# Column scores of a pooled attention on Trainium2: eight one-row transposes of a copied row in place of eight products, and new orders on four engines

## What is computed

```python
x = x + L0(x)   # zX*laplace_x + zY*laplace_y + zR*x*(1-x), per-batch scalars, reflected borders
x = x + L1(x)   # pooled attention, below
x = x + L2(x)   # x @ W[subject].T + b[subject], W one of eight 512x512
x = x + L3(x)   # adapter: z = relu(x@Wd + bd); y = x + z@Wu + bu; layer norm * g + b

def L1(hidden):
    attn_in = tanh(einsum('bsd,da->bsa', hidden, W1) + b1)     # a = 128
    scores = einsum('bsa,a->bs', attn_in, v)                   # one score per row of x
    mask = l <= j, l >= j or l != j, by the batch's token      # 1024 x 1024
    p = softmax(where(mask, scores[:, None, :], -1e30), axis=-1)
    return einsum('bjl,bld->bjd', p, hidden) / count(mask)
```

## Time and profile before

| | us |
|---|---|
| median of 3 runs | 558.15 |
| lowest, highest run | 556.75, 558.15 |
| the profiled execution, whole | 555.42 |
| its span in the trace | 553.6 |
| TensorE busy | 530.6 (96%) |
| VectorE busy | 467.9 (85%) |
| ScalarE, GpSimd busy | 312.3, 311.0 (56% each) |
| mean share of full TensorE clock granted | 0.992 |

### The profile page before, as it was taken

One profiled execution on the slowest core, in us unless ns is written; L12 is line 12 of the kernel. 1 busy time (PEld: TensorE's weight loads), 2 busy tenths in 40 slices (PEclk: granted clock), 3 DMA queues, 4 the chain that ended last, 5 costly groups with the idle time before them and its releaser, 6 DMA issues.

```text
span 553.6 us, 8994 instructions
## 1 busy us (share of the span) xinstructions
PE 530.6 (96%) x2838; PEld 417.1 (75%) x2838; DVE 467.9 (85%) x1164; ACT 312.3 (56%) x545; POOL 311.0 (56%) x283
## 2 busy tenths in 40 slices
PE   8996789999999999999999999999999999999995
PEld 3565576988688876888778885888778886888783
DVE  6548795999799997999889996999979998787677
ACT  5644663477635774576654775367655676335520
POOL 5156713597266944598275962589355872246241
PEclk9997999999999999999999999999999999999999
DMA  7974665585997579973898659965998847422563
GB/s 249 312 191 76 180 219 171 109 175 103 282 308 163 114 190 318 261 140 102 260 317 189 143 142 313 269 141 106 236 331 194 171 98 212 58 58 57 115 90 120
DMA packets 63942, 100.83 MB, mean 182 GB/s; under 512 B 10894, under 2 KB 16526, under 8 KB 63895
## 3 DMA queue, kind: packets, MB, share of 16 engines
q0 software_dynamic: 16544, 29.90, 33.0%
q1 hardware_dynamic: 38096, 53.54, 30.2%
q10 hardware_dynamic: 9254, 16.81, 8.0%
HBM read 67.43 MB, written 31.98 MB: 180 GB/s over the span
## 4 chain that ended last, share of the span: by engine, by line
PE 84%; DVE 7%; ACT 4%; issue 3%; POOL 1%; DMA 1%; ACTq 0%; DVEq 0%
PE y L697 37%; PE front_ps L755 10%; PE front_ps L836 8%; PE front_ps L697 6%; PE front_ps L778 5%; PE front_ps L711 4%; PE front_ps L763 3%; PE front_ps L769 2%; PE front_ps L800 2%; DVE x2f L1555 2%; ACT zh L1140 2%; DVE pn L1509 1%; PE front_ps L810 1%; PE front_ps L782 1%; PE y L737 1%
## 5 line engine op out<-in xcount | busy, mean ns | idle before, releaser
L583 POOL TENSOR_TENSOR norm<-norm 128x1 f32<-128x1 f32 x64 | 51.3, 801 | 150.5 <-DVE norm L1582 149.7
L697 PE MATMUL y<-wth,x2h 128*128 128x512 f32 x256 | 104.0, 406 | 0.0
L697 PE MATMUL y<-wth,x2l 128*128 128x512 f32 x256 | 100.2, 392 | 0.0
L697 PE MATMUL y<-wtl,x2h 128*128 128x512 f32 x256 | 100.0, 391 | 0.0
L601 POOL TENSOR_TENSOR x2l<-x2f,x2h 128x1024 fp32r<-128x1024 f32 x32 | 76.8, 2400 | 14.6 <-ACT x2h L1017 14.4
L564 POOL TENSOR_TENSOR xd<-xn 128x1024 f32<-128x1024 f32 x28 | 54.7, 1954 | 44.2 <-DVE x L1428 22.7
L1555 DVE SCALAR_TENSOR_TENSOR x2f<-alb,small,front_ps 128x128 f32<-128x128 f32 x256 | 70.7, 344 | 1.7 <-POOL x2l L601 0.4
L836 PEld LDWEIGHTS front_ps<-th_pt,x 128*128 128x128 f32 x512 | 62.0, 190 | 6.9 <-DVE x2f L1555 4.1
L836 PE MATMUL front_ps<-th_pt,x 128*128 128x129 f32 x512 | 64.7, 278 | 2.5 <-DVE x2f L1555 1.0
L590 POOL DMA_DIRECT2D out<-o_sb x58 | 57.1, 1056 | 8.1 <-ACT o_sb L1157 7.1
L1017 ACT ACTIVATE x2h<-x2f 128x1024 fp32r<-128x1024 f32 x32 | 34.0, 1062 | 46.6 <-DVE x2f L1555 46.6
(11 more groups left out here) (138 smaller groups left out, 1092.3 us busy)
## 6 DMA issues: line engine op xcount, KB each, us to landing
xn<-in_x SPq DMA_DIRECT2D x32, 512.0 KB, 7.7
out<-x ACTq DMA_DIRECT2D x58, 256.0 KB, 4.0
out<-o_sb POOLq DMA_DIRECT2D x58, 256.0 KB, 6.4
xu<-in_x SPq DMA_DIRECT2D x21, 512.0 KB, 7.8
xu<-in_x POOLq DMA_DIRECT2D x21, 512.0 KB, 7.6
wn_wd<-in_L_cond_weight SPq DMA_DIRECT2D x8, 1024.0 KB, 6.6
wn_wd<-in_L_cond_down_w SPq DMA_DIRECT2D x8, 256.0 KB, 6.6
up_row<-in_L_cond_up_b SPq DMA_DIRECT2D x8, 256.0 KB, 4.3
```

The lines of the kernel that those rows point to most:

```text
L583: pool.tensor_tensor(rstd[:, r:r + 1], ve[:, r:r + 1], minus_half[:, :], ALU.pow).then_inc(rstd_ready, 1)
L697: ins = mm(dst, lhs, rhs, start=first and q == 0, stop=last and q == len(parts) - 1, skip_group_check=True)
```

## The change

`scores_by_row` no longer multiplies. ScalarE copies the first partition of the spread scores, 1 by 512 for each half, from PSUM into the first partition of `th`, once VectorE has read that half (`sb_read`), so `th` is no longer needed there; TensorE turns the row into eight columns, with a 1x1 identity, once both halves are copied (`score_kept`). In `steady` it comes one `linear` later than before. All four compute engines' lists are written in a new order, in `opening`, `first`, `steady` and `last`; no other step changes what it does, and SyncE's list stays in its order (a helper only takes the test for the last batch).

```diff
+        score_kept = sem("score_kept")
...
             def scores_by_row(n):
-                pe.wait_ge(th_ready, 2 * n + 2)
+
+                pe.wait_ge(score_kept, 2 * n + 2)
                 for j in range(NJ):
-                    ins = mm(SN[:, j:j + 1], th[:, blk(j)], v_col[:, :], start=True, stop=True)
+                    ins = pe.transpose(SN[:, j:j + 1], th[0:1, blk(j)], ident[0:1, 0:1])
                 ins.then_inc(sn_ps, 1)
...
+            def keep_scores(n, h):
+
+                act.wait_ge(sb_read, 2 * n + h + 1)
+                copy(th[0:1, half(h)], pair_b[0:1, half(h)]).then_inc(score_kept, 1)
```

TensorE, the lists of `opening`, `steady` and `last`:

```diff
                 spread_scores(0, 0)
                 spread_scores(0, 1)
                 scores_by_row(0)
+                block_sums(0)
                 down_through_w(0)
-                block_sums(0)
                 transpose_p(0, 0)
...
                 linear(b, 1 - q, 7)
+                adapter_up(b, 1 - q, 6)
                 transpose_w(n, 0)
-                adapter_up(b, 1 - q, 6)
                 adapter_down(n, q)
                 adapter_up(b, 1 - q, 7)
+                if m is not None:
+                    transpose_x1(m, 1 - q, 0)
                 transpose_w(n, 1)
-                if m is not None:
-                    transpose_x1(m, 1 - q, 0)
                 transpose_w(n, 2)
...
                     spread_scores(m, 0)
                     spread_scores(m, 1)
+                linear(n, q, 2)
+                if m is not None:
                     scores_by_row(m)
-                linear(n, q, 2)
+                linear(n, q, 3)
                 if m is not None:
                     block_sums(m)
                     down_through_w(m)
-                linear(n, q, 3)
+                adapter_up(n, q, 2)
                 if m is not None:
                     transpose_p(m, 0)
-                adapter_up(n, q, 2)
...
                 adapter_up(LAST, 1, 5)
+                linear(LAST, 1, 7)
                 adapter_up(LAST, 1, 6)
-                linear(LAST, 1, 7)
                 adapter_up(LAST, 1, 7)
```

ScalarE, the start and the middle of `steady`, and its end:

```diff
+                small_exps(n)
                 if m is not None:
                     reflect(m, 0)
-                small_exps(n)
+                row_exps(n)
+                store_base(b, 2)
+                round_v(n)
+                seed(b, 4)
+                keep_p(n, 0)
+                keep_p(n, 1)
...
                 adapter_relu(n, 1)
+                store_base(b, 7)
                 round_w(n, 1)
                 round_w(n, 2)
...
-                store_base(b, 6)
-                store_base(b, 7)
...
                     hidden(m, 1)
+                    keep_scores(m, 0)
                 scale(n, 0)
                 if m is not None:
+                    keep_scores(m, 1)
```

More of the change, by code:

```diff
@@ L609, in first @@
             def first():
-                rest_difference(0)
+                start_sum(0)
                 add_below(1, 0)
+                rest_up(0, 0)
                 add_below(1, 1)
@@ L616, in first @@
                 add_below(1, 2)
-                add_below(1, 3)
                 left_and_right(1, 2)
-                start_sum(0)
-                rest_up(0, 0)
+                rest_difference(0)
                 rest_x2(0, 0, 0)
@@ L624, in first @@
                 rest_x2(0, 0, 3)
+                add_below(1, 3)
                 left_and_right(1, 3)
@@ L628, in steady @@
             def steady(b, n, m, q):
+                start_sum(n)
+                rest_up(n, q)
                 if m is not None:
                     left_and_right(m, 0)
+                rest_difference(n)
+                if m is not None:
                     add_below(m, 0)
                     add_below(m, 1)
+                finish(b, 0)
                 root(b, 1)
-                finish(b, 0)
+                if m is not None:
+                    add_below(m, 2)
+                root(b, 2)
                 if m is not None:
                     left_and_right(m, 1)
-                rest_up(n, q)
-                root(b, 2)
-                rest_difference(n)
-                if m is not None:
-                    add_below(m, 2)
-                start_sum(n)
+                    add_below(m, 3)
+                rest_x2(n, q, 0)
                 root(b, 3)
                 finish(b, 1)
-                rest_x2(n, q, 0)
-                if m is not None:
-                    add_below(m, 3)
+                rest_x2(n, q, 1)
                 finish(b, 2)
                 root(b, 4)
-                rest_x2(n, q, 1)
+                finish(b, 3)
                 if m is not None:
@@ L1223, in first @@
                 centre(1, 2)
+                scale_rows(1, 3)
+                centre(1, 3)
+                store_base(0, 0)
                 keep_x1t(1, 1, 0)
-                centre(1, 3)
-                seed(0, 1)
                 keep_x1t(1, 1, 1)
@@ L1274, in steady @@
                 if m is not None:
-                    scale_rows(m, 3)
+                    scale_rows(m, 2)
+                store_base(b, 6)
+                scale(b, 4)
                 round_x2(n, q, 3)
@@ L1687, in steady @@
                 subtract_mean(b, 1 - q, 1)
-                keep_x3(b, 2)
+                keep_x3(b, 3)
                 row_weights(n)
+                probabilities(n, 0)
+                rest_v(n)
                 adapter_bias(n)
-                rest_v(n)
-                probabilities(n, 0)
                 probabilities(n, 1)
-                keep_x3(b, 3)
                 moments(b, 2)
@@ L1747, in steady @@
                 subtract_mean(b, 1 - q, 7)
+                keep_x3(n, 0)
                 if m is not None:
@@ L1751, in steady @@
                     diffuse(m, 1 - q, 2)
-                keep_x3(n, 0)
-                if m is not None:
                     times_x(m, 3)
```

174 lines of the change are left out of this document (86 added, 88 removed).

## The result

The changed kernel took 571.42 us (median of 6 runs, 565.68 to 573.74), the kernel before 557.29 beside it; the ratio is 1.0239, interval 1.0186 to 1.0292. It is **slower by 2.4%**, where 550.2 was forecast.

A forecast was written before the change was run, and what follows sets the result against it. TensorE, busy 96% of the span, was taken as the bound. Savings of 4.1 (score block), 1.5 (boundary waits), 1.0 (opening) and 1.2 us (last batch) sum to 7.8, giving 550.2 against a 558.15 median; range 545.5 to 556.0.

The forecast's parts named there:

- the other swaps: Remaining reorderings on all engines: move 0.5 to 1 us of work under covers of about 1 us, counted as 0.
- Rival (b): At the softmax's 8-column VectorE operation, GpSimd's hold lasts its whole run: +13 us, 563; chance 0.07 with similar waits.
- The opening: Batch 0's start: add_around after four probabilities instead of eight, so -1.0 us, bounds -2 and +1.
- Rival (d): TensorE's clock falls in the opening, before down_through_w: 552 us, inside the forecast's range and its 0.66 chance.
- The early start_sum and rest_up: GpSimd does these sums early, while it idled, shortening the hold on the softmax's 8-column operation to 0.3 from 3 us.
- The last batch: TensorE's idle before adapter_up(7, 1) shrinks because stores are issued earlier: -1.2 us, bounds 0 and -2.1.
- the boundary: Stretch between batches, spread scores to first pooling product: about 14.5 us instead of 15.46.
- The score block: Eight one-row transposes on TensorE take 1.1 us instead of 1.68, saving 0.58 at each of seven boundaries, 4.1 in all.
- The copies: ScalarE's two score copies are done during linear(2), with 0.65 us to spare, so transposes do not wait outside the opening.
- The row that was L1494: Sign: VectorE's 8-column operation in the softmax, 3.07 us before, should take under 0.6 us.
- the waits at `pn`: TensorE's waits for p before its transposes: five of 0.35 us go, seven of 0.05 come, counted as -1.5 us.

The follow-up runs named there:

- a_around: Changed kernel with VectorE's add_around(m, 1) put back ahead of subtract_mean(b, 5) in the steady passes: 555.8 us, ratio 0.9964 to the kernel before.
- a_exps: Changed kernel with the opening's small_exps(0) put back ahead of reflect(1, 0) and reflect(1, 1) on ScalarE: 566.2 us, ratio 1.0144.
- c_ident: Changed kernel with the add_around and small_exps(0) swaps both undone and add_identity moved behind maxima on VectorE: 548.1 us; 548.2, ratio 0.983, in more rounds.
- a_both: Changed kernel with both the add_around and the small_exps(0) swaps undone: 551.6 us, ratio 0.9868 to the kernel before.
- c_prod: c_ident with the old eight fp32 column-score products in place of the one-row transposes, without the two copies: 555.1 us, ratio 0.9961.
- a_gap: Changed kernel with one more GpSimd wait, for its own root, between root(b, 5) and rest_x2(n, 3): 555.9 us, ratio 0.9985.

## Why the prediction was wrong

**The step that failed** is the sentence "the other swaps ... counted as 0, and they cost what they exceed this by". Among the swaps on VectorE one is not in that sum at all, add_around behind subtract_mean. It moved an operation of 1.3 us by 0.7 us and cost 15.6 us in the runs (a_around). The forecast knew the mechanism: it used it to explain L1494 and took it as an upside. It would have had to be applied to every VectorE operation with two SBUF inputs, in the new order against GpSimd's new order. Rival (b) was this mechanism at one place, the wrong one, and had 0.07.

**The opening**: -1.0 was forecast with bounds of -2 and +1; the first pooling product came at 53.98, before at 49.70, so it was +4.3. The missed term is the hold of L1488 behind the reflections moved ahead of small_exps(0); with them back behind it the product came at 50.7 (a_exps; 49.9 and 50.5 in the two profiles of c_ident's kernel), and the time of a_both is 4.2 below that of a_around. Rival (d), the fallen clock, came true as well, and stayed in c_ident: 0.50 in the window 40 to 42.

**The early start_sum and rest_up** were read as work of GpSimd "while it idled", without VectorE's operations of that moment. They hold add_identity when a load lands late: with it moved away the median is 5.6 us lower (571.4 against 565.8).

**The last batch**: -1.2 was forecast from an idle that TensorE did not have; 0 is right. The step is the reading of the earlier trace rows.

**What held**: the boundary. The score block was taken as 1.1 with a lower bound of 0.88 and is 0.58, so the block is 1.1 shorter at a boundary and not 0.58; c_prod puts its worth at 0.98 a pass. The lower bound came from transposes in which 128 columns move, while here one does; the eight bias products of down_through_w, one column each, took 0.79 (227.60 less 226.81, from the earlier trace rows), and were the nearer row. The copies were covered by linear(2) in every pass where nothing was held. The row that was L1494 ran in 0.15 us, and the waits at `pn` went. With the three holds out, c_ident took 548.1, close to the 550.2 forecast, but by errors that cancel, which is luck: the block is worth 6.9 us (c_prod) where 4.1 was forecast, and all the orders together 1.8 (c_prod against the 556.9 of the kernel before beside it) where 1.5 + 1.0 + 1.2 was.

## What to carry to other kernels

When an order changes, list the VectorE operations with two SBUF inputs and the GpSimd operations beside them, before and after: a VectorE operation that comes ahead of a run of GpSimd instructions goes first (1.3 us), one that comes 0.1 us behind the first of them waited for the whole run here (4.7 us). Where VectorE is the more urgent, a wait of GpSimd for its own last instruction, put between two of a run, lets it in. And read whose idle time an "issue" in the chain is before counting it for the engine that bounds the kernel.

## What the runs showed of the hardware

- GpSimd instructions that follow each other without standing at a wait kept VectorE's two-input operation out over the whole run, not over one instruction: 3.52 us with the end of root and rest_x2 ahead, 4.67 with root and rest_x2, 5.36 with 256 columns more, 1.27 with a wait in between at which GpSimd stands. Waits that were already met did not end a run: two stand between root and rest_x2 in the 4.67, and one more in the 5.36.
- The Trainium skill (SBUF — State Buffer, section "SBUF: two separate sides") speaks of a lock for one instruction. By that VectorE would here have been let in when root ended, at 262.51, and have been done by 263.8; it was done at 265.97.
- L1488 began at 37.45 and the first sum of GpSimd at 37.76, with a DMA issue of GpSimd before it. Whether the issue kept VectorE out for those 0.3 us is open; spans on GpSimd are rough.
- With the wait of a_gap in place even root, which began 0.1 us before add_around, did not hold it; root's own span grew to 1.78 us, from the 0.55 that it takes alone. Why the short instruction gives way and the run does not is open.
- A one-row transpose starts 0.06 us after the one before it (1.07 for sixteen, 0.58 for eight), a full one 0.11 (0.88 for eight). A 64-row product took 0.43 between full ones where 0.24 is usual; the eight one-row transposes of one column between 512-column products had 0.1 over their spacing at the start and 0.04 at the end.
